# Three DRAINs more on GpSimd in the tail, and where the scatters of a mixture-of-experts layer wait

## The reference, cut to what matters

```python
scores = x @ gate_w.T                                   # 1024 tokens, 8 experts
mult, sel = _masked_sampling_omp(scores)                # two experts and weights a token
h = silu(einsum('th,efh->etf', x, w1)) * einsum('th,efh->etf', x, w3)
y = einsum('etf,ehf->eth', h, w2)
coef = (one_hot(sel, 8) * mult[..., None]).sum(axis=1)
out = einsum('te,eth->th', coef, y)
x = x + tanh(g_ffn[1]) * out
```

## Time and profile before

| | us |
|---|---|
| median of 3 runs | 220.32 (219.25 to 220.54) |
| the profiled execution | 220.97 |
| its span, first to last instruction | 218.9 |
| PE busy in the span | 202.9 |
| POOL busy in the span | 85.8 |

### The profile page before, as it was taken

How to read it: one execution, slowest core, us unless ns; L and a number is a source line. 1 busy time by engine, 2 the same in 40 slices (tenths; PEclk the granted TensorE clock), 3 DMA queues, 4 the chain that set the end, 5 groups by cost and what they waited for, 6 DMA issues and landing times.

```text
span 218.9 us, 3823 instructions
## 1 busy us (share of the span) xinstructions
PE 202.9 (93%) x1282; PEld 158.8 (73%) x1282; DVE 134.5 (61%) x461; ACT 85.6 (39%) x188; POOL 85.8 (39%) x107
## 2 busy tenths in 40 slices
PE   8999979999999998998989999999999999999920
PEld 7787854435785346787979998999973599999910
DVE  4598697999988969997888495853317601111200
ACT  2678661998200646034343263222226322222100
POOL 8175316620001020054640343543877556443222
PEclk9999999999999999999999999999999999999985
DMA  5748418129999125817142221322332311022322
GB/s 170 199 192 250 114 40 260 53 70 371 413 420 417 42 68 188 315 50 237 41 139 101 27 25 24 49 41 44 66 71 26 71 13 9 7 24 27 43 25 23
DMA packets 16795, 26.07 MB, mean 119 GB/s; under 512 B 4094, under 2 KB 12421, under 8 KB 16774
## 3 DMA queue, kind: packets, MB, share of 16 engines
q1 hardware_dynamic: 11328, 20.14, 25.5%
q0 software_dynamic: 4064, 5.25, 13.7%
q10 hardware_dynamic: 1382, 0.41, 1.0%
HBM read 21.34 MB, written 5.51 MB: 123 GB/s over the span
## 4 chain that ended last, share of the span: by engine, by line
PE 35%; DVE 29%; DMA 14%; issue 9%; ACT 7%; POOL 3%; DVEq 1%; POOLq 0%; ACTq 0%
PE PS L2081 13%; DMA out_dram<-a,ids_late 9%; PE PS L2113 6%; DMA out_dram<-zb,sidx 4%; PE PS L1784 3%; PE PS L2124 3%; DVE stat L1070 3%; DVE hT L1462 3%; ACT a L841 2%; PE PS L1848 2%; DVE work L1148 2%; DVE x L1322 1%; DVE mv L1077 1%; PE PS L1835 1%; DVE work L1134 1%
## 5 line engine op out<-in xcount | busy, mean ns | idle before, releaser
L2081 PE MATMUL PS<-hT,e 128*128 128x128 f32 x512 | 62.0, 276 | 1.1 <-ACT hT L970 1.1
L2081 PEld LDWEIGHTS PS<-hT,e 128*128 128x128 f32 x512 | 60.1, 192 | 2.9 <-ACT hT L970 1.9
L1966 PE MATMUL PS<-xnT,e 128*128 128x512 f32 x88 | 39.6, 598 | 1.9 <-DVE hT L1462 1.1
L1966 PEld LDWEIGHTS PS<-xnT,e 128*128 128x128 f32 x88 | 16.1, 190 | 22.1 <-issue 17.4
L1718 DVE TENSOR_TENSOR hT<-th,PS 128x512 f32<-128x512 f32 x15 | 10.3, 687 | 35.4 <-PE PS L2081 29.3
L2113 PE MATMUL PS<-e,hT 128*128 128x256 f32 x128 | 30.6, 382 | 0.2 <-DVE x L1500 0.2
L2113 PEld LDWEIGHTS PS<-e,hT 128*128 128x128 f32 x128 | 23.1, 190 | 2.8 <-issue 0.3
L646 POOL TENSOR_TENSOR rstd<-veps,nhalf 128x2 f32<-128x2 f32 x12 | 8.7, 726 | 39.7 <-DVE veps L1079 39.6
L709 POOL DMA_INDIRECT out_dram<-a,ids_early x8 | 12.9, 1607 | 24.4 <-ACT a L1004 11.4
L1980 PE MATMUL PS<-e,hT 128*128 128x256 f32 x96 | 21.7, 383 | 0.0
L1980 PEld LDWEIGHTS PS<-e,hT 128*128 128x128 f32 x96 | 17.9, 190 | 2.9 <-issue 0.5
(11 more groups left out here) (301 smaller groups left out, 318.5 us busy)
## 6 DMA issues: line engine op xcount, KB each, us to landing
e<-e_in SPq DMA_DIRECT2D x24, 512.0 KB, 8.7
x<-x_in SPq DMA_DIRECT2D x2, 512.0 KB, 6.4
graph_rows<-e SPq DMA_DIRECT2D x4, 256.0 KB, 2.1
out_dram<-x SPq DMA_DIRECT2D x4, 256.0 KB, 2.5
xn_rows<-xn SPq DMA_DIRECT2D x4, 256.0 KB, 2.4
e<-gw_in SPq DMA_DIRECT2D x1, 768.0 KB
e<-uw_in SPq DMA_DIRECT2D x1, 640.0 KB
e<-dw_in SPq DMA_DIRECT2D x1, 640.0 KB
```

What stands on the lines that cost most here:

```text
L1966: mm = pe.matmul(PS[:, bank, :], w[:, k, it * P:(it + 1) * P], xnT[:, h, k, :], start=(k == 0), stop=(k == 1))
L2081: mm = pe.matmul(PS[:, bank + q, f * P:(f + 1) * P], w[:, k * F + f * P:k * F + (f + 1) * P], xgT[x_at][:, k, :], start=(k == 0), stop=(k ...
```

## The change

A second `("retire",)` is put at the end of `POOL_ORDER`, after the gathers 14 and 15 and ahead of the reading of the number of pairs. Two further DRAINs stand after the scatters 11 and 14. The scatters 10 to 15 count their landings in a semaphore of their own, `late_scattered`. The scatters 11 to 15 wait for constant values of it; only scatter 10 still computes a value from the number of pairs. And `pool.sem_inc(pool_passed)` is left out of all static scatters but the tenth.

```diff
@@ gpsimd's list
-                      ("gather", 14), ("gather", 15)]
+                      ("gather", 14), ("gather", 15), ("retire",)]
@@ SyncE's last wait
-            sp.wait_ge(last_scattered, 16)
+            sp.wait_ge(late_scattered, 16 * (STATIC - AT))
@@ scatter(j)
                 pool.wait_ge(y_scaled, j + 1)
-                if j >= AT:
+                if j == AT:
                     pool.wait_ge(scattered, pairs * 64 + 16 * j)
+                    pool.sem_inc(pool_passed)
+                elif j > AT:
+                    pool.wait_ge(late_scattered, 16 * (j - AT))
                 elif j:
                     pool.wait_ge(scattered, 16 * j)
-                pool.sem_inc(pool_passed)
                 pool.indirect_dma_start(
...
-                    .then_inc(last_scattered if j == STATIC - 1 else scattered, 16)
+                    .then_inc(late_scattered if j >= AT else scattered, 16)
@@ after the loop
             for j in range(AT, STATIC):
                 scatter(j)
+                if j in (STATIC - 5, STATIC - 2):
+                    pool.drain()
```

More of the change, by code:

```diff
@@ L394, in build @@
         scattered = sem("scattered")
-        last_scattered = sem("last_scattered")
+        late_scattered = sem("late_scattered")
         CONSTS = 23
```

## The result

| | before | changed |
|---|---|---|
| median, us | 220.15 (18 runs) | 221.0 (18 runs) |
| ratio, changed to before | | 1.0042 (95%: 1.0023 to 1.0062) |
| the profiled execution's span | 218.9 | 218.9 |

The change makes the kernel slower by 0.9 us (0.5 to 1.4), well within 1%. Two of the changed kernel's 18 runs (223.22 and 224.37) lie over 1.5% above its fastest and are left out of the ratio. The forecast was +0.45 us, 220.7. The two spans look alike only because the changed kernel's execution was 0.6 us quicker before the part that changed: its first overflow result was ready at 173.97 + 0.47 = 174.44 us, that of before at 175.07. From it to the span's end there were 218.89 - 175.06 = 43.8 us before and 218.87 - 174.44 = 44.4 after: +0.6 us in this pair of executions.

What follows compares the result with a forecast made beforehand. Bound from 175.99 us by a chain of scatters, each awaiting the previous landing, then GpSimd's last DRAIN. 0.7 + 0.37 + 0.16 - 0.78 = +0.45 us; median put at 220.7 us, range 219.2 to 222.4.

Steps and rivals of the forecast that it cites:

- The price of a DRAIN: GpSimd's DRAINs behind indirect DMAs: end after the last landing by 0.043 us for each transfer since the DRAIN ahead.
- hidden retirement: Rival: DRAINs work off the backlog beside the last transfer, only the rest shows; -0.4 us, 219.9; chance 0.33.
- fixed price: Rival: every DRAIN overhangs by 1.05 us whatever has piled up; +3.5 us, 223.8; chance 0.17.
- cost nothing: Rival: DRAINs only wait for GpSimd to be idle, last one unchanged; 0 us, 220.3; chance 0.05.
- The DRAIN ahead of the loop: Before the overflow loop, covering 12 transfers: first overflow scatter and chain late by 0.7 us, bounds 0.2 to 1.3.
- After scatter 11 and after 14: Two tail DRAINs, covering 8 and 3 transfers: cost 0.37 and 0.16 us, each between 0.05 and 1.1.
- The last DRAIN: At the kernel's end, now covering one transfer: overhang falls from 1.03 to 0.04 us, giving 0.78 back; then SyncE sets the end.
- The waits: On the static scatters: landing's wait stays ahead of the DMA, worth 0; four earlier scatters start up to 0.53 us sooner, worth 0.
- The rival of the shorter links: Landing's wait met with the DMA already decoded: 0.53 us off five links, -2.65 us, 218.1 with the forecast's +0.45; chance 0.07.

Runs made afterwards that it cites:

- the seven counts: Overhangs of DRAINs after 1, 3, 8, 12, 20, 24 and 26 transfers, from several kernels: 0.08, 0.16, 0.37, 0.53 and 0.54, 0.87, 1.04, 1.11 us.
- the repetition: Second measurement of the change's waits without its three DRAINs, landing's wait on the DMA for scatters 11 to 15: 217.45 us, ratio to before 0.9894.
- hidden DRAIN: Kernel before plus one DRAIN in the loop's first half, after the index copies' issue: ratio 0.9988; two candidate runs, adding landing's wait on the DMA: 0.985, 0.986.
- waits alone: Changed kernel without its three new DRAINs, keeping the late scatters' semaphore and left-out increments (two instructions fewer ahead): ratio to before 0.9999.
- landing's wait on the DMA: As waits alone, but scatters 11 to 15 have the landing's wait written first, so it sits on the DMA: ratio to before 0.9858.
- two more: Changed kernel with two more increments of the unused semaphore pool_passed early in GpSimd's program: ratio to before 1.0098, from 4 runs.
- one more: Changed kernel with one more increment of the unused semaphore pool_passed early in GpSimd's program: ratio to before 1.0015.
- one fewer: Changed kernel without the DRAIN ahead of the loop, keeping the tail's two: ratio to before 0.9999.
- the loop DRAIN alone: Kernel before with only the DRAIN ahead of the loop added: ratio 1.0025, +0.55 us.

## Why the prediction was right, point by point

- **The price of a DRAIN** (proportional to the transfers, 0.043 us each, behind the last landing): right where only landings are open, 0.041 and 0.04 fixed. Two DRAINs of 26 and 24 transfers could not tell it from a fixed price; the seven counts above do. The rivals "hidden retirement", "fixed price" and "cost nothing" fall with them.
- **The DRAIN ahead of the loop**, forecast to make the chain late by 0.7 us: 1.64 - 0.92 = 0.72. The scatter started 2.57 us behind the DRAIN's end (176.08 - 173.50), forecast 2.6. That the index copies would take 0.42 and not 1.4 us once VectorE was idle held too (0.43). No run shows why they are slower beside VectorE's.
- **After scatter 11 and after 14**, 0.37 and 0.16: the links are longer by 0.40 and 0.14 than those of before (5.00 against 4.60, 4.71 against 4.57).
- **The last DRAIN**, 0.78 back: from the last landing to the span's end it is 0.46 us now (218.87 - 218.41) and was 1.27 (218.89 - 217.62), 0.8 back, and SyncE sets it now, as forecast.
- **The waits**: nothing in the tail, as forecast, with the landing's wait still ahead of the DMA (0.76 us from landing to start, 0.79 before); alone they gave 0.9999. The earlier scatters did start sooner, to no effect. Scatter 5 started 0.28 us behind its result (ready at 143.55 + 0.47 = 144.02, start 144.30), 0.83 before (144.64 and 145.47).
- **What the sum left out** is the stretch of one link, 0.3 us, which came with moved code. With it +0.45 becomes +0.75, inside the measured 0.5 to 1.4; without it the forecast lay just under the interval. The prediction had no term for moved code. The profiled pair differs by 0.6 in the tail: 0.7 at the first overflow scatter, 0.75 in the links, 0.75 back behind the last start, and 0.1 less in the overflow scatters, where nothing was changed.
- **How much the number proves.** Little by itself: hidden retirement (219.9) and no cost (220.3) lay in the range of 219.2 to 222.4 as well. The terms read from the trace decide. The prediction held 1% for about what a measurement can tell; the interval here is 0.2% to each side.
- **The rival of the shorter links** was rightly unlikely for this change and was the largest effect to be had in this stretch. Its forecast was -2.65 us; five links gave -2.66 once the waits were put that way. It takes the 0.52 us from 0.79 to 0.27 at each start, 2.6 in all; that the sums agree to 0.01 is luck, as the repetition had 20.4 us for its five links.

## What to carry to other kernels

In a chain of transfers that wait for each other, look which instruction holds the wait that ends last. Here a start came 0.27 us behind the landing with that wait on the DMA itself and 0.76 with it on an instruction ahead, and the order of two lines decided it. Put a DRAIN where something else is late anyway, and count which instructions of the sequencer then stand behind it. Here each transfer since the last DRAIN cost 0.041 us at one DRAIN or another: the one hidden DRAIN took 0.5 us off the last overhang (1.04 to 0.54) and left the first overflow scatter 0.95 us behind its result (0.92 before), while the change with its three DRAINs is slower by 0.9. A difference of a few tenths of a microsecond can go with where code lies, as the 0.3 to 0.4 us of the stretch did, so shift it by an instruction before explaining it. And when a chain has become shorter, look again at the lead of what feeds it (here 2.4 us before, 0.5 to 0.9 after).

## What the runs showed of the hardware

- A DRAIN of GpSimd with nothing but indirect DMAs ahead ended 0.04 us + 0.041 us for each of them after the last had landed, from 1 transfer (0.08 us, changed kernel) to 26 (1.11, every kernel). Idle time ahead of the landing did not hide it: at 24 transfers, in the kernel before, GpSimd's last work ended at 215.45, 2.2 us ahead of the landing at 217.62, and the 1.04 us still came behind. With index copies between the last gather and the DRAIN it was 0.68 to 0.72 us for 12 transfers (the three kernels with the hidden DRAIN) instead of 0.53.
- From a landing to the next static scatter's start, with no DRAIN between and no stretch, there were 0.76 to 0.81 us with the wait on an instruction ahead and 0.27 to 0.30 with it on the DMA. The sequencer's next instruction behind the last scatter began 0.49 us after the wait-only instruction's end (waits alone) and 0.04 us after the landing (landing's wait on the DMA).
- One scatter of the tail started 0.3 to 0.4 us late in six kernels: 13 in the changed one, 14 with two instructions fewer ahead, 12 with two more, none with one more or one fewer; 12 with the loop DRAIN alone and with the hidden one, 14 in the repetition of the landing's wait on the DMA. Each time an 8 KB transfer of the kind `instruction` began within 0.25 us of the scatter's start.
- Three one-column copies of GpSimd took 1.4 us beside VectorE's 128 x 1024 copies (171.80 to 173.20, kernel before) and 0.43 without them (174.63 to 175.06, changed kernel).
